# Graph attention on one core: the neighbour sort of a tile goes in front of the next tile's wait for exponentials

## The reference, cut to what matters

```python
h = einsum('nf,fhd->nhd', layernorm(x), W)                  # graph attention, 8 heads of 32
e = leaky_relu(a_src[src] + a_dst[dst], 0.2)
e_exp = exp(e - segment_max(e, dst)[dst])
alpha = e_exp / (segment_sum(e_exp, dst)[dst] + 1e-16)
x = x + relu(segment_sum(h[src] * alpha, dst) + bias)
x = x + ffn_of_best_expert(layernorm(x))                    # 32 experts of 64 units, top 1
t = einsum('ni,rio->rno', layernorm(x), weight)             # 16 relations
x = x + segment_sum(t[edge_type, src] * edge_weight, dst)
x = x + moe_ffn(layernorm(x))                               # 8 experts, top 2, layer norm at the end
```

## Time and profile before

| what | value |
|---|---|
| median of three runs | 3035.34 us |
| span of the profiled execution | 4112.2 us |
| granted TensorE clock over the span | 0.810 of full |
| busy: PE, DVE, ACT, POOL | 2666.3, 2101.8, 871.8, 1823.8 us |
| attention layer in the profile | about 180 to 2310 us |
| its hardware loop (20 pairs) | about 406 to 2159 us |

### The profile page before, as it was taken

How to read it: one execution, slowest core, us unless ns; L and a number is a source line. 1 busy time by engine, 2 the same in 40 slices (tenths; PEclk the granted TensorE clock), 3 DMA queues, 4 the chain that set the end, 5 groups by cost and what they waited for, 6 DMA issues and landing times. The chain is left out here.

```text
span 4112.2 us, 40174 instructions
## 1 busy us (share of the span) xinstructions
PE 2666.3 (65%) x9189; PEld 1725.2 (42%) x9189; DVE 2101.8 (51%) x5260; ACT 871.8 (21%) x1741; POOL 1823.8 (44%) x1896
## 2 busy tenths in 40 slices
PE   2525677778777777666688555354746545558897
PEld 2424444455445444444456332133433333335665
DVE  4787555666556565555575213425443443423176
ACT  1311222222222222122232112111211111112331
POOL 4455443344434444444432543555554455442054
PEclk7757788889888888777899777677877777779899
DMA  5642333333333333333332336433333333322222
GB/s 160 160 126 71 106 107 106 105 115 104 110 111 112 110 102 112 107 101 104 104 114 87 119 122 216 149 101 111 106 115 97 98 101 97 96 81 82 76 90 75
DMA packets 263686, 448.63 MB, mean 109 GB/s; under 512 B 52138, under 2 KB 154466, under 8 KB 263586
## 3 DMA queue, kind: packets, MB, share of 16 engines
q0 software_dynamic: 84608, 232.41, 20.8%
q1 hardware_dynamic: 148162, 186.82, 13.2%
q10 hardware_dynamic: 30816, 28.32, 2.0%
HBM read 279.75 MB, written 167.63 MB: 109 GB/s over the span
## 5 line engine op out<-in xcount | busy, mean ns | idle before, releaser
L885 POOL DMA_INDIRECT gat_rows<-h_table,idx x799 | 788.8, 987 | 1030.5 <-DVEq L1335 799.9
L1143 PE MATMUL bank<-tr_wr,tr_xt 128*128 128x512 f32 x1568 | 782.7, 639 | 328.0 <-ACT tr_row L990 130.0
L1639 POOL DMA_INDIRECT rel_rows<-transformed,rel_idx x655 | 621.7, 949 | 658.9 <-DVEq L1892 431.4
L1143 PEld LDWEIGHTS bank<-tr_wr,tr_xt 128*128 128x128 f32 x1568 | 315.0, 205 | 651.7 <-issue 440.6
L1694 PE MATMUL bank<-ex_xt,ex_w 128*128 128x512 f32 x768 | 402.6, 654 | 269.7 <-ACT ex_ht L1770 218.0
L1106 PE MATMUL bank<-mo_xt,mo_w 128*128 128x256 f32 (+1 forms) x1600 | 454.5, 405 | 137.6 <-issue 92.7
L990 ACT ACTIVATE tr_row<-bank 128x512 f32<-128x512 f32 x392 | 232.9, 597 | 1211.6 <-remote 696.5
L1703 PE MATMUL bank<-ex_w,ex_ht 128*128 128x256 f32 x1536 | 388.2, 401 | 130.1 <-ACT ex_ht L1770 95.3
L1124 PE MATMUL bank<-mo_w,mo_ht 128*128 128x256 f32 x1568 | 401.1, 397 | 51.9 <-issue 51.4
L1703 PEld LDWEIGHTS bank<-ex_w,ex_ht 128*128 128x128 f32 x1536 | 311.8, 204 | 261.0 <-issue 120.3
L1106 PEld LDWEIGHTS bank<-mo_xt,mo_w 128*128 128x128 f32 x1600 | 307.9, 206 | 264.0 <-issue 180.5
(11 more groups left out here) (347 smaller groups left out, 2724.4 us busy)
## 6 DMA issues: line engine op xcount, KB each, us to landing
transformed<-tr_row SPq DMA_DIRECT2D x392, 256.0 KB
ys<-ex_y ACTq DMA_DIRECT2D x192, 128.0 KB
gat_rows<-h_table,idx POOLq DMA_INDIRECT x799
rel_rows<-transformed,rel_idx POOLq DMA_INDIRECT x655
ex_w<-L_ffn_W SPq DMA_DIRECT2D x16, 512.0 KB
h_table<-hrow SPq DMA_DIRECT2D x49, 132.0 KB, 1.9
records<-xa SPq DMA_DIRECT2D x49, 132.0 KB
partial<-ne_sum SPq DMA_DIRECT2D x49, 128.0 KB, 2.0
```

The costliest lines, as they stand in the source:

```text
L885: pool.indirect_dma_start(out=rows[:, column(u, j), :], out_offset=None, in_=p.h_table[:], in_offset=bass.IndirectOffsetOnAxis(ap=idx[u][: ...
L1143: ins = pe.matmul(p.bank[6 + c % 2][:], xt2[:, k, u * P:(u + 1) * P], wr[:, k, m * CW:(m + 1) * CW], start=(k == 0), stop=(k == KD - 1))
L1639: pool.indirect_dma_start(out=rows[:, column(u, j), :], out_offset=None, in_=p.transformed[:], in_offset=bass.IndirectOffsetOnAxis(ap=idx[ ...
```

## The change

The call of `ordered` leaves the end of `tile`. Each `tile` but the first now calls `ordered(t - 1)`, for the tile before, right in front of its wait for the exponentials, behind `lagged(i)` where that stands. The last tile's sort is called after the last tile. The same sorts run, 49 of them, on the same engine.

```diff
@@ tile @@
                     lagged(i)
                 if u == 1 and early and i == 2:
                     choose(1)
+                if not (isinstance(i, int) and i == 0 and u == 0):
+                    ordered(t - 1)
                 dve.wait_ge(p_ready, 1)
                 dve.sem_inc(p_ready, -1)
@@ end of tile @@
                 chain.back(LAST_STEPS if i is PAIRS else STEPS)
-                ordered(t)
@@ after the loop @@
             in_pairs(dve, pair, LAG)
             tile(PAIRS, 0, 2 * PAIRS)
+            ordered(2 * PAIRS)
             dve.sem_inc(late_ready, 1)
```

## The result

| kernel | median | range, runs | ratio to before |
|---|---|---|---|
| before | 3035.32 us | 3034.7 to 3038.03, 4 | |
| changed | 3069.69 us | 3068.35 to 3070.97, 4 | 1.0109 [1.0095, 1.0123] |

The change costs 34 us by these medians. The profiled execution of the changed kernel took 3068.35 us with a span of 3066.6 us at a clock of 0.911. It has none of the holes of the earlier trace rows, so it can't be set against the profile of before as it stands (4112.2 us). I therefore profiled the kernel before a second time: span 3037.1 us, clock 0.912. All comparisons from here on use that execution, which is called *before, profiled again*.

What follows compares the result with a forecast made beforehand. DVE's own work was taken to bound the kernel in the pairs concerned. New gather waits of 31.8 us less 7.3 given back, with the sort and the end at 0, gave +24.5 on 3035.3, say 3060 us; range 3026 to 3069.

Steps and rivals of the forecast that it cites:

- The profile's holes: Idle time in the profile, 475 us on PE in the attention loop, taken as a profiling cost the runs mostly lack.
- DVE sets the pace: Attention loop: DVE's work is longest in the named pairs, 65 to 69.5 us against PE's 59 to 64.
- rival C: Attention loop: ACT waits for scores and holds PE up, so earlier scores shorten the ring; 2960 us, chance 0.07.
- The moved sort, at 0: DVE, before the exponentials' wait: the 7.4 us sort runs 49 times either way, so its work changes by 0.
- The late gathers, at 31.8: DVE, before the scores: gathers from column 16 on lose the sort's cover; new waits in ten tiles, 31.8 us.
- The give-back, at -7.3: DVE's norms behind tiles 8 and 10: waits of 4.46 and 2.86 us for ACT's square root go, -7.3 us.
- The end, at 0: Last tiles: tile 48's sort stays, tile 47's delays a sum as much as scores came earlier; 0 on DVE's row.
- this lead: Lagged work reaches PE 7.4 us earlier: worth up to 7.4 us once, 0 where DVE sets the pace.
- The signs to look for: In the trace after: gather waits of 1 to 7 us, L1305 shrinks, L1240 grows as much, tile 8's 4.46 us gone.
- A: Attention loop: PE and ACT set the pace, late gathers vanish in DVE's slack, PE starts 7.4 us earlier; 3027.9 us, chance 0.24.
- B: Nothing to measure: late gathers and lead cancel, or gathers land faster in the runs; 3035 us, chance 0.14.
- D: Tiles with u = 0: sort behind lagged delays sums, norms and PE's transposes, up to 5.5 us a pair; 3145 us, chance 0.05.

Runs made afterwards that it cites:

- the 12 shared columns: 12 instead of 16 columns shared by the two tiles in flight, in both kernels: before so edited 3033.84 us, changed so edited 3042.38 us.
- the doubled comparison: Kernel before with the sort's 32 by 32 comparison issued twice in each of the 49 tiles, nothing moved: 3095.07 us (1.0192).
- The reverse order, sort first: Changed kernel, but in tiles of u = 0 the sort stands ahead of the lagged work instead of behind it: 3080.54 us (1.0141).

## Why the prediction was right, point by point

The time forecast was 3060, the time measured 3069.7. The mechanism was the one forecast, and the sum was 10 us short. The median lies 0.7 us above the top of the range in us, 3069, which stood for all late gathers with nothing given back; by the ratio 1.0109 the change makes it 3068.4. So the largest term was right, and of the terms put beside it none was.

- **The profile's holes.** Right: profiled again, the kernel has none, and its span is 3037.1 us. Counting DVE's work in a pair instead of taking over the 220.7 us of L1305 was the step that saved the forecast. Without the holes it is 2.4 us.
- **DVE sets the pace.** Right. 61.7 us more of DVE made 56.9 us more of time. But the statement that ACT never waited for scores in the loop was wrong. It waited 278.6 us in 43 cases; the 91.9 us of the earlier trace rows were another effect of the holes. This speaks for the premise, not against it. It also shows why rival C failed though part of its condition was met: ACT waits for scores, but DVE waits only 2.4 us for ACT's exponentials, so scores sooner brought no gain.
- **The moved sort, at 0.** Mis-sized. The same instructions take the same time, but the changes at the edges don't cancel. DVE now starts the weighing 0.26 us late behind the sort's last step (L1316, +11.0 us in all); the start of the sort gives 7.2 back, and L1399 takes 2.5. From the first mask to the end of the last sort DVE takes 1539.9 us before and 1581.4 after, +41.5, of which 34.9 are gathers. About 6.6 us are left for these edges. With the 12 shared columns it is the same: 1533.0 and 1550.7, +17.7, of which 9.4 are gathers, and 8.3 are left.
- **The late gathers, at 31.8.** Right in place and nearly in size. Predicted and measured new waits, tile by tile: 9: 7.4 and 7.2; 11: 6.2 and 6.2; 13: 3.7 and 3.7; 15: 2.4 and 2.7; 36: 0.7 and 0.9; 38: 0.7 and 0.9; 40: 1.9 and 3.1; 42: 3.2 and 4.3; 43: 1.2 and 1.2; 44: 4.4 and 4.7. The sum is 34.9. All even tiles came out longer than reckoned. Why was not tested; the gathers of the undisturbed execution were on average longer than those of the profile with holes, from which the landing was reckoned (1125 against 987 ns, L885).
- **The give-back, at -7.3.** This is the step that failed. The square-root waits of 4.46 and 2.86 us behind tiles 8 and 10 were those of the profile with holes. In the undisturbed one L1258 waits 0.46 us behind each of these two tiles, before and after, and 44.8 us in 27 places before and 44.4 after; nothing went. I had declared the waits of that profile unfit to be taken over, and then took over two of them.
- **The end, at 0.** Wrong as well, by -8.7. PE's matmul comes 32.0 us later where DVE's last sort comes 40.7 later. Of this 6.2 us are the experts' choice, which now stands ahead of a sort; the other 2.5 are a faster last pair of PE, whose cause stays open. The prediction had named this lead and given it 0 wherever DVE sets the pace. It is worth something all the same, once, because before it was PE that ended the phase; in the changed kernel the two come level.
- **The sum as it came out.** Gathers 34.9, edges 6.6, the end -8.7: 32.8, against a difference of 29.5 between the spans, 34 between the first medians and 32 against the later ones of before. The two terms put at 0 (edges, end) nearly cancel, which is luck, and the give-back, at -7.3, is most of what the sum was short.
- **The signs to look for.** The gathers' waits came in each of the named tiles. L1305's wait did not shrink, as it was hardly there (2.4 us), and L1240's grew by 2.1 us only, from 7.0 to 9.1. Tile 8's long wait wasn't gone; it was never in the runs.
- **The rivals.** A fell by the doubled comparison, B by the result. D didn't come: in the changed kernel PE's transposes (L1061) waited for norms in seven pairs where they had not before, but by 0.2 to 3.2 us, not by 5.5 in each of 20. The reverse order, sort first, is the slower one (by 8.5 to 10.9 us).
- **The holes once more.** In the loop of before, profiled again, PE is busy for 1206.67 of 1290 us, so idle for 83 us against the 475 from the earlier trace rows:

```profile
370.00:1660.00 1290.00, 1206.67 (x4523) 787.23 (x4522) 1059.72 (x2423) 426.05 (x837) 890.53 (x776) 0.98 0.50 148
```

ACT's longest standstill in that stretch has a named releaser, DVE's scores of tile 10, which stand behind the seven summing slots of tile 9; the 17.24 us "remote" of the earlier trace rows have no counterpart:

```profile
452.12 0.67 ACT L940 ACTIVATE gat_rows<-gat_score 128x256 f32<-128x256 f32 x1 [13.01 <-DVE gat_score L1288]
```

The Trainium skill, page "Runtime: NRT & Kernel Launch", section "Instruction fetch mechanics", says that a taken branch to a target outside the two pages held forces a fetch. If the 17 us had been such a fetch at the loop's end, they would stand in this trace too, which has the same loop; it shows none of this size. Whether the loop's start lies outside those pages on ACT, no run here shows.

## What to carry to other kernels

Work that stands in front of a wait may be its cover: before moving it, ask what lands while it runs, and compare what it moves past with what it leaves. Here a sort of 7.4 us was the cover of late gathers in ten of 49 tiles, and the wait that it was to fill was 2.4 us in the whole kernel. A profiled execution that is a third longer than the runs can mislead in any wait of one engine for another (220.7 us for exponentials in it, 2.4 without the holes); if only that one is to be had, count the work on each engine, or profile again. And where one engine sets the pace of a loop but another ends it, the order in which the first serves the second within a step can be worth several microseconds once (6.2 here).

## What the runs showed of the hardware

- The same kernel, profiled twice, had spans of 4112.2 and 3037.1 us with the same busy time on DVE (2101.8 and 2101.0 us) and ACT (871.8 and 871.3), but 2666.3 and 2463.6 on PE, whose clock was 0.810 in the first and 0.912 in the second, and 1823.8 and 1954.0 on POOL, where a gather took 987 ns on average in the first and 1125 in the second. In the profiled executions of the other kernels here the span was 1.7 to 2.0 us below the execution's own time, and that time within 4 us of the kernel's median.
- Waits of 0.26 us in front of an instruction whose semaphore had long been counted up: where the sort stands right in front of that wait, the weighing starts 0.26 us late in nearly every tile (13.4 us in 49). With only the odd or only the even tiles moved it is 7.8 and 7.0 us, so about half, and the kernel with the sort in front of the gathers, below, shows 1.2 us. That it is the end of the sort's chain that costs, and not its place, was not tested apart.

```profile
L1316 DVE TENSOR_TENSOR gat_rows<-gat_rows 128x1024 f32<-128x1024 f32 (+1 forms) x169 | 254.3, 1528 | 1.2 <-DVEq L1307 1.2
```
